# Block attention on one Trainium2 core: weight products from fp32 to three float32r products, with the weights split on the chip

## The chip, the core and the metric

One core of a Trainium2 chip runs one program. The time is the device time of one execution in microseconds; lower is better. TensorE (PE) multiplies and transposes, VectorE (DVE) and ScalarE (ACT) do elementwise work and empty the accumulation banks (PSUM), GpSimd (POOL) subtracts and issues some DMAs, SyncE (SP) issues the other DMAs.

## What is computed

Eight batches of 256 rows x 512 features, all in fp32. Layer 0 is a cross attention over features with mean and deviation outputs; the change leaves its instructions as they are. Then a transformer block of self attention, cross attention and MLP, cut to what matters here:

```
ln_out = layernorm(hidden_states, ln1_s, ln1_b)
qkv = ln_out @ w_qkv + b_qkv                     # 512 x 1536
ctx = attention(q, k, v, ltor_mask)              # 16 heads of 32
h = hidden_states + ctx @ w_ao + b_ao            # 512 x 512
q2 = layernorm(h, ln2_s, ln2_b) @ w_q + b_q      # cross: q from h
kv = encoder_states @ w_kv + b_kv                # k and v from the context
h = h + attention(q2, k2, v2, cross_mask) @ w_co + b_co
out = h + gelu(layernorm(h) @ w1 + b1) @ w2 + b2
```

## The kernel before

`build` calls `layer0`, `attention` and `mlp`. `attention` makes 16 runs in a row: run 0 to 7 are the self attention of batch 0 to 7, run 8 to 15 their cross attention. A run has 16 steps (m); a step is the scores of two heads for 128 queries. Each engine has its own instruction stream, written out by hand in this order of steps, and they meet at semaphores only.

TensorE, per step m: it waits for the exponentials of step m (`s_exp`), issues the scores of step m+2, transposes the probabilities of step m (`turn`), and on even steps multiplies them with v (`pv`). In steps 2 and 3 it transposes the normalized rows of the next run (`turn_x`), after steps 5, 9, 13 and 15 the reciprocal sums (`turn_sums`). What is left of a step carries half an `item`. Items are the weight products: q, k and v of the next run and the output product of the previous run, two items each (n = 0, 1), eight a run. Each item fills the one bank IB, which must be emptied before the next item starts (`s_free`). Before: v1 at m=1, out0 at 3, out1 at 5, q0 at 7, k0 at 9, q1 at 11, k1 at 13, v0 at 15 (part 0 of an item is done in the step before its m). Item products are fp32 matmuls: q and k 4 x 128x128 weights against 256 rows per half (L870); v with 128 rows as weights against 256 columns of the weight matrix, so that v item n covers half of the features of both row blocks (L875); out with 128 rows of `heads` against 512 columns (L883).

VectorE, per step m: `maxima` of step m+2 (L961 and two L966, which also leave the row maxima), copies of `probT` at m%4=0, reciprocals at m%4=3, `layer_norm` at m=0, `values` (v plus bias), `residual` at m=3 and 5 (L1002, L1004), `keep_rows` at m=5 and 7 (L76 to L81: statistics of the new rows and their copies into X and moments), `high_parts` (L989) of a q or k item, and the division by the sums into `heads` (L1070). Before a cross run it makes `off` from the mask in two dependent instructions (`mask_off`, L948, L950).

ScalarE, per step m: the exponentials of step m+1 (L1083), `probT` copies in the other steps, `take_x` at m=2 and 3 (L1106: scale and bias of the layer norm, bank to `xT`), `take` of a q or k item (L1097), and the spreading of the reciprocal sums (L1115, L1122).

POOL subtracts the high part of each q or k item from the whole (L1175) and issues four DMAs per item; SP issues eight (L785). These DMAs build `q_stack` and `k_stack`, 96 rows of high and low parts, from which `scores` is one float32r matmul (L823). The stacks of item n=1 are first needed by the scores of step 8. SP also loads weights and masks: `w_cross` as 4 MB and eight masks in run 0.

The MLP already uses float32r: each fp32 product is three products of high parts and rests (L1272 with 256 moving columns, L1285 with 512), with the weights split on ScalarE (L1320), VectorE (L1361) and POOL (L1349).

Of the kernel before, what the change touches and what calls it, by code (L numbers as in the profile page):

```python
# [7 lines left out]
F32 = mybir.dt.float32  # L8
# [6 lines left out]
P = 128  # L15
NB = 8
# [55 lines left out]


def keep_rows(eng, links, g, batch, s, rows, six, two):

    eng.bn_stats(six[:], rows).then_inc(links.sem, 1)  # L76
    eng.wait_ge(links.sem, links.after())
    eng.tensor_scalar(g["X"][:, batch, s, :], rows, 1.0, None, ALU.mult)
    eng.bn_aggr(two[:], six[:]).then_inc(links.sem, 1)
    eng.wait_ge(links.sem, links.after())  # L80
    eng.tensor_scalar(g["moments"][:, batch, s, :], two[:], 1.0, None, ALU.mult).then_inc(links.sem, 1)  # L81
    eng.wait_ge(links.sem, links.after())
# [18 lines left out]
def layer0(nc, d, g):  # L101
# [25 lines left out]
    with ExitStack() as ctx:  # L127
# [95 lines left out]
        with nc.Block() as block:  # L223
            @block.sync
            def _(eng):
# [25 lines left out]
                for dst, src in ((g["gb"], d["gb"]), (g["b_feat"], d["b_feat"]), (g["b1"], d["b1"]),  # L251
                                 (g["w_self"], d["w_self"])):
                    eng.dma_start(dst[:], src).then_inc(s_big, DMA)
# [418 lines left out]
def attention(nc, d, g):  # L672
# [5 lines left out]
    AHEAD = [("q", 0), ("k", 0), ("v", 0), ("q", 1), ("k", 1)]  # L678

    def weights_of(run):  # L680

        w, wo = (g["w_self"], g["wo_self"]) if run < NB else (g["w_cross"], g["w_cross"][:, :, 3 * D:4 * D])
        return {"q": w[:, :, 0:D], "k": w[:, :, D:2 * D], "v": w[:, :, 2 * D:3 * D], "out": wo}

    def item_at(run, m):

        if m == 1 and run < RUNS:
            return ("v", 1, run)
        if m in (3, 5) and run:
            return ("out", m // 5, run - 1)  # L690
        at = {7: ("q", 0), 9: ("k", 0), 11: ("q", 1), 13: ("k", 1), 15: ("v", 0)}
        if m in at and run + 1 < RUNS:
            return at[m] + (run + 1,)
        return None

# [4 lines left out]
    with ExitStack() as ctx:  # L700
# [6 lines left out]
        mask = sb("mask", [P, NB + 1, SB, S])  # L707
        off = sb("off", [P, SB, S])
        ctxT = sb("ctxT", [P, DC, S])
        xn = sb("xn", [P, SB, D])  # L710
        xT = sb("xT", [P, DC, S])
# [4 lines left out]
        v = sb("v", [P, SB, D])  # L716
# [8 lines left out]
        heads = sb("heads", [P, NG, S])  # L725
        part = sb("part", [P, D])
        six = sb("six", [P, 6])
        two = sb("two", [P, 2])
# [3 lines left out]
        s_w = sem("w")  # L732
        s_in = sem("in")
# [6 lines left out]
        s_x = sem("x")  # L740
        s_item = sem("item")
# [20 lines left out]
        s_link = sem("link")  # L762

# [29 lines left out]
        with nc.Block() as block:  # L793
            @block.sync
            def _(eng):
# [728 lines left out]
```

## Time and profile before

| | us |
|---|---|
| median of 3 runs (lowest to highest) | 1943.78 (1942.11 to 1946.71) |
| profiled execution, its own time | 1945.68 |
| its span | 1943.9 |
| TensorE busy (matmuls) | 1811.0, 93% |
| VectorE busy | 1300.8, 67% |
| ScalarE busy | 993.7, 51% |
| GpSimd busy | 346.2, 18% |

The attention runs from about 760 to 1550 us of the span. Times in rows are microseconds from the start of the span unless marked ns. PE is the matmuls, PEld the weight loads, which overlap them; the ends of matmuls are modelled, so the distance from start to start is the surer measure. A name such as `L870` is a line of the kernel before. Merged rows of a timeline show how many records they hold (x8).

### The profile page before, as it was taken

How to read it: one execution, taken by the hardware profiler on the slowest of the kernel's cores; microseconds unless marked ns; L12 is line 12 of the kernel's file. 1: busy time of each engine (PE TensorE's matmuls, PEld its weight loads, DVE VectorE, ACT ScalarE, POOL GpSimd, SP SyncE). 2: the span in 40 equal slices, each digit the busy share in tenths (PEclk: the TensorE clock that was granted, in tenths of full speed). 3: DMA queues.
4: the chain of work that ended last, by engine and by line, in shares of the span. 5: the costliest groups of instructions: out<-in, count | busy, mean ns of one | idle time of the engine just before them, and what ended most of it. 6: DMA issues, size and time to landing. Idle time of an engine off the chain costs nothing. (4 is left out here: it accounts for less than half of the span.)

```text
span 1943.9 us, 32814 instructions
## 1 busy us (share of the span) xinstructions
PE 1811.0 (93%) x11744; PEld 1179.6 (61%) x11744; DVE 1300.8 (67%) x2733; ACT 993.7 (51%) x2227; POOL 346.2 (18%) x397
## 2 busy tenths in 40 slices
PE   6999999999999982899999999999999879999998
PEld 2333333333333321777777777777777569999998
DVE  4678788887878731688888788788888653333332
ACT  1555665655666551566666666666666552111111
POOL 0001112111112113322223232222222040000000
PEclk7899999999999975999999999999999989999999
DMA  3001011110100001722232223233333050000000
GB/s 150 31 16 46 14 46 27 35 49 13 48 14 26 27 13 68 234 63 69 68 73 72 62 72 81 67 80 79 77 81 83 8 173 18 11 11 11 11 11 22
DMA packets 71936, 104.93 MB, mean 54 GB/s; under 512 B 21104, under 2 KB 35952, under 8 KB 71152
## 3 DMA queue, kind: packets, MB, share of 16 engines
q1 hardware_dynamic: 63600, 86.27, 15.7%
q0 software_dynamic: 8192, 16.79, 3.6%
q8 instruction: 83, 1.36, 0.3%
q14 instruction: 61, 0.50, 0.1%
HBM read 39.55 MB, written 4.72 MB: 23 GB/s over the span
## 5 line engine op out<-in xcount | busy, mean ns | idle before, releaser
L427 DVE TENSOR_REDUCE nmax<-ps 128x2 f32<-128x1024 f32 x256 | 311.3, 1220 | 137.4 <-PE ps L325 136.4
L559 ACT ACTIVATE prob<-ps 128x1024 f32<-128x1024 f32 x256 | 261.7, 1022 | 226.0 <-PE ps L337 225.7
L1083 ACT ACTIVATE at_prob<-at_t,at_nmax 128x256 f32<-128x256 f32 x512 | 255.7, 503 | 180.0 <-DVE at_nmax L966 178.2
L352 PE MATMUL ps<-prob,v 128*64 128x512 f32 x1024 | 287.1, 640 | 0.0
L966 DVE CUSTOM_DVE_ANT_0 at_t<-at_t,at_off 128x256 f32<-128x256 f32 x512 | 229.8, 485 | 8.8
L325 PE MATMUL ps<-k,q 32*128 32x512 f32 x1024 | 196.1, 462 | 18.3 <-DVE k L415 7.9
L325 PEld LDWEIGHTS ps<-k,q 32*128 32x128 f32 x1024 | 84.8, 191 | 193.1 <-issue 109.9
L961 DVE SCALAR_TENSOR_TENSOR at_t<-ps,at_mask 128x512 f32<-128x512 f32 x256 | 175.0, 683 | 31.3 <-PE ps L823 28.7
L1337 ACT ACTIVATE mlp_h<-ps,b 128x256 f32<-128x256 f32 x128 | 53.7, 472 | 269.4 <-PE ps L1272 269.2
L1376 DVE CAST mlp_h_hi<-mlp_h 128x512 fp32r<-128x512 f32 x64 | 29.3, 458 | 220.9 <-ACT mlp_h L1337 220.9
L1175 POOL TENSOR_TENSOR at_low<-at_low,at_high 128x512 fp32r<-128x512 f32 x64 | 81.4, 1271 | 515.7 <-DVE at_high L989 450.2
L823 PE MATMUL ps<-at_k_stack,at_q_stack 96*128 96x256 f32 x512 | 153.4, 382 | 10.6 <-ACT at_prob L1083 9.8
L835 PE MATMUL ps<-ident,at_prob 128*128 128x128 f32 x1024 | 155.7, 274 | 1.1 <-ACT at_prob L1083 1.1
L1272 PE MATMUL ps<-mlp_x_hi,mlp_w_hi 128*128 128x256 f32 x512 | 145.6, 284 | 7.5 <-DVE mlp_w_lo L1361 7.5
L1272 PE MATMUL ps<-mlp_x_lo,mlp_w_hi 128*128 128x256 f32 x512 | 145.6, 284 | 0.0
L1272 PE MATMUL ps<-mlp_x_hi,mlp_w_lo 128*128 128x256 f32 x512 | 145.5, 284 | 0.0
L337 PE MATMUL ps<-q,k 32*128 32x512 f32 x512 | 131.4, 509 | 11.0 <-ACT prob L559 10.7
L870 PE MATMUL ps<-at_xT,w_self 128*128 128x256 f32 x512 | 128.7, 397 | 6.1 <-ACT at_low L1097 3.4
L835 PEld LDWEIGHTS ps<-ident,at_prob 128*128 128x128 f32 x1024 | 119.4, 141 | 1.6 <-ACT at_prob L1083 1.6
L823 PEld LDWEIGHTS ps<-at_k_stack,at_q_stack 96*128 96x128 f32 x512 | 92.1, 192 | 44.0 <-issue 22.8
L1149 ACT ACTIVATE at_probT<-ps 128x512 f32<-128x512 f32 x192 | 111.6, 581 | 7.8 <-PE ps L835 7.8
L352 PEld LDWEIGHTS ps<-prob,v 128*64 128x64 f32 x1024 | 51.9, 138 | 98.0 <-issue 97.1
(138 smaller groups left out, 3496.3 us busy)
## 6 DMA issues: line engine op xcount, KB each, us to landing
at_k_stack<-at_high SPq DMA_DIRECT2D x256, 64.0 KB, 2.1
at_q_stack<-at_high SPq DMA_DIRECT2D x128, 64.0 KB, 2.7
at_q_stack<-at_high POOLq DMA_DIRECT2D x128, 64.0 KB, 2.4
at_q_stack<-at_low SPq DMA_DIRECT2D x128, 64.0 KB, 2.3
at_k_stack<-at_low POOLq DMA_DIRECT2D x128, 64.0 KB, 2.3
mlp_w_in<-in_w SPq DMA_DIRECT2D x32, 256.0 KB, 3.0
c_in<-in_ctx SPq DMA_DIRECT2D x8, 512.0 KB, 4.2
X<-in_x SPq DMA_DIRECT2D x8, 512.0 KB, 4.9
```

Of the source, the lines that this page charges most:

```text
L325: mm = eng.matmul(ps[:, SC + 2 * (N % 2) + i, :], lhsT[r, slot, P * j:P * (j + 1)], rhs[r, n % RING, :], start=(half == 0), stop=(half == 1))
L337: mm = eng.matmul(ps[:, ST + i, :], lhsT[r, n % RING, P * c:P * (c + 1)], rhs[r, slot, :], start=(half == 0), stop=(half == 1))
L352: mm = eng.matmul(ps[2 * QD * k:2 * QD * (k + 1), VB, :], v[:, c, HG * G + 2 * p + k, :], prob[:, M % PROBS, k, :], start=(c == 0), stop=( ...
L427: eng.tensor_reduce(nmax[:, n % 2, j, 2 * p:2 * p + 2], ps[:, at:at + 2, :], AX, ALU.max, negate=True).then_inc(s_max, 1)
L559: eng.activation(prob[:, M % PROBS, :, :], ps[:, ST:ST + 2, :], ACT.Exp).then_inc(s_exp, 1)
L823: mm = eng.matmul(ps[:, SC + p, S * i:S * (i + 1)], q_stack[:, 2 * p + i, T, P * j:P * (j + 1)], k_stack[:, 2 * p + i, T, :], start=True, ...
L835: mm = eng.transpose(ps[:, PT + m % 2, P * k:P * (k + 1)], prob[:, m % 2, i, P * c:P * (c + 1)], ident[:])
L870: mm = eng.matmul(bank[:, S * T:S * (T + 1)], w[:, c, P * (2 * n + T):P * (2 * n + T + 1)], src[:, c, :], start=(c == 0), stop=(c == DC - 1))
L961: eng.scalar_tensor_tensor(out=t[:, i, :, :], in0=ps[:, SC + i, :].rearrange("p (h k) -> p h k", h=2), scalar=-SCALE, in1=mask[:, mask_of( ...
L966: ins = eng.tensor_tensor_reduce(t[:, i, k, :], t[:, i, k, :], off[:, j, :], 1.0, NEVER, ALU.add, ALU.min, nmax[:, m % 4, k:k + 1])
L1083: ins = eng.activation(prob[:, m % 2, i, :], t[:, p, i, :], ACT.Exp, scale=-1.0, bias=nmax[:, m % 4, i:i + 1], accum_out=z[:, T % 2, j, 2 ...
L1272: mm = eng.matmul(ps[:, HB + n % 2, S * i:S * (i + 1)], w[:, c, col], x[:, c, :], start=(k == 0), stop=(k == len(terms) - 1))
```

## The change

- Products of q, k, v and out become float32r: W x = W_hi x_hi + W_hi x_lo + W_lo x_hi (`TERMS`), three matmuls for one. In run 0 the q, k and v products stay fp32 (`whole`).
- v is made by token blocks: item n is 128 rows against all 512 columns, and `v` has two buffers, one for each parity of the run.
- Weights: ScalarE copies the fp32 weights to `w_hi` (which rounds them), VectorE writes `w_lo = w_raw - w_hi` over `w_raw`, in pieces of 128 x 512 placed by `pieces_at`. Self weights are split in run 0, q, k and v of the cross weights in run 7 and their out weights in run 8. The cross weights are loaded over the self weights' rests, by role and after the last self item of that role.
- Activations: `take_x` writes `x_hi` and the whole x (over `xn`), `low_x` the rest; the context is split by `high_context` and `low_context`, the head outputs by `high_heads` and `low_heads`.
- Order of items: k1 at m=1 of its own run, out0 3, out1 5, q0 7, k0 9, v0 11, v1 13, q1 15.
- `keep_rows` goes: `residual` writes X in place, `statistics` writes `moments` directly. `mask_off` is one instruction. Masks have two buffers instead of nine and are loaded one per cross run.
- The DMA of the self out weights comes behind the first stacks.

```diff
-    AHEAD = [("q", 0), ("k", 0), ("v", 0), ("q", 1), ("k", 1)]
+    AHEAD = [("q", 0), ("k", 0), ("v", 0), ("v", 1), ("q", 1)]
+    TERMS = ((0, 0), (0, 1), (1, 0))
...
+    def pieces_at(run, m):
+
+        if run in (0, NB - 1) and m in (3, 4, 5, 6, 8, 9):
+            role, c = {3: (0, 0), 4: (0, 2), 5: (1, 0), 6: (1, 2), 8: (2, 0), 9: (2, 2)}[m]
+        elif run in (0, NB) and m in (10, 11):
+            role, c = 3, 2 * (m - 10)
+        else:
+            return []
+        return [(0 if run == 0 else 1, role, c), (0 if run == 0 else 1, role, c + 1)]
...
+                        if name == "out":
+                            eng.wait_ge(s_hlo, NG * run + 2)
+                        if name == "q":
+                            eng.wait_ge(s_x if run == 0 else s_xlo, 2 if run == 0 else 2 * run)
+                        if name == "k" and run >= NB:
+                            eng.wait_ge(s_clo, 2 * (run - NB) + 2)
...
-                                mm = eng.matmul(bank[:, S * T:S * (T + 1)], w[:, c, P * (2 * n + T):P * (2 * n + T + 1)],
-                                                src[:, c, :], start=(c == 0), stop=(c == DC - 1))
...
+                                for k, (a, z_) in enumerate(TERMS):
+                                    mm = eng.matmul(out, w[a][:, c, col], src[z_][:, c, :],
+                                                    start=(c == 0 and k == 0), stop=(c == DC - 1 and k == 2))
...
+                            for k, (z_, a) in enumerate(TERMS):
+                                mm = eng.matmul(bank, src[z_][:, c, rows], w[a][:, c, :],
+                                                start=(c == 0 and k == 0), stop=(c == DC - 1 and k == 2))
...
+                def low_x(run, n):
+
+                    eng.wait_ge(s_x, 2 * run + n + 1)
+                    half = slice(2 * n, 2 * n + 2)
+                    eng.tensor_tensor(x_lo[:, half, :], xn[:, :, S * n:S * (n + 1)], x_hi[:, half, :].bitcast(F32),
+                                      ALU.subtract).then_inc(s_xlo, 1)
...
+                def low_weights(layer, role, c):
+
+                    if layer == 0 and c == 0 and role < 3:
+                        made(eng, ROLES[role], 1, 0)
+                    eng.wait_ge(s_whi, 4 * (4 * layer + role) + c + 1)
+                    eng.tensor_tensor(weights(1, role)[:, c, :], weights(2, role)[:, c, :],
+                                      weights(0, role)[:, c, :].bitcast(F32), ALU.subtract).then_inc(s_wlo, 1)
...
+                        if m in (4, 5) and run + 1 < RUNS:
+                            low_x(run + 1, m - 4)
+                        if m in (6, 7) and NB <= run + 1 < RUNS:
+                            low_context(run + 1, m - 6)
+                        if m in (0, 1) and run:
+                            low_heads(run - 1, 2 + m)
+                        if m in (8, 12):
+                            low_heads(run, m // 4 - 2)
+                        if m:
+                            for x in pieces_at(run, m - 1):
+                                low_weights(*x)
...
+                    for c in range(2 * n, 2 * n + 2):
+                        for dst in (x_hi[:, c, :], raw_x(c))[run == 0:]:
+                            ins = eng.activation(dst, ps[:, TB, S * (c % 2):S * (c % 2 + 1)], ACT.Identity,
+                                                 bias=gb[:, 1, c:c + 1], scale=gb[:, 0, c:c + 1])
...
+                        if m in (5, 6) and NB <= run + 1 < RUNS:
+                            high_context(run + 1, m - 5)
+                        if m in (7, 11, 15):
+                            high_heads(run, m // 4 - 1)
+                        if m == 0 and run:
+                            high_heads(run - 1, 3)
+                        for x in pieces_at(run, m):
+                            high_weights(*x)
```

On SP, the loads of the cross weights (four DMAs of 256 KB for each role) stand between and behind the stacks of run 7: q's between the stacks of q1 and k1, k's and v's behind k1's; the out weights' stand in front of the stacks of run 9.

## Rows read from the trace of the kernel before

**Rows 1.** The page's forty slices, matmuls, busy tenths.
```profile
PE   6999999999999982899999999999999879999998
```
**Rows 2.** Stretches: from:to, length, busy PE, PEld, DVE, ACT, POOL, granted clock, DMA.
```profile
971.30:1017.80 46.50, 46.38 (x355) 36.77 (x353) 38.31 (x112) 30.33 (x96) 12.96 (x21) 1.00 0.29 69
...
1308.20:1355.90 47.70, 46.48 (x355) 36.85 (x354) 39.34 (x114) 30.35 (x96) 13.03 (x21) 1.00 0.32 78
...
786.90:831.50 44.60, 39.81 (x295) 33.20 (x295) 32.39 (x97) 28.60 (x89) 14.75 (x22) 0.96 0.71 225
```
**Rows 3.** Waits in one self run: who waited for whom, us, times, longest.
```profile
ACT at_prob L1083 <- DVE at_nmax L966: 11.0, 8, 2.4
```
**Rows 4.** Timeline of TensorE in self runs: start, us, engine, line, operation.
```profile
961.31 2.00 PE L870 MATMUL ps<-at_xT,w_self 128*128 128x256 f32 x8
...
962.96 0.59 PE L823 MATMUL ps<-at_k_stack,at_q_stack 96*128 96x256 f32 x2
...
985.87 0.81 PE L823 MATMUL ps<-at_k_stack,at_q_stack 96*128 96x256 f32 x2
...
987.82 0.19 PEld L883 LDWEIGHTS ps<-wo_self,at_heads 128*128 128x128 f32 x1 [0.24 <-issue]
...
988.25 0.19 PEld L883 LDWEIGHTS ps<-wo_self,at_heads 128*128 128x128 f32 x1 [0.24 <-issue]
...
994.80 0.48 PE L823 MATMUL ps<-at_k_stack,at_q_stack 96*128 96x256 f32 x2
```
**Rows 5.** Timeline of TensorE in the MLP, float32r products of 256 and 512 columns.
```profile
1742.27 0.28 PE L1272 MATMUL ps<-mlp_x_hi,mlp_w_hi 128*128 128x256 f32 x1
...
1745.15 0.63 PE L1285 MATMUL ps<-mlp_w_hi,mlp_h_hi 128*128 128x512 f32 x2
...
1747.89 0.28 PE L1272 MATMUL ps<-mlp_x_hi,mlp_w_hi 128*128 128x256 f32 x1
```
**Rows 6.** VectorE groups, 740 to 1480 us: busy, mean ns, idle before them.
```profile
L1070 DVE TENSOR_TENSOR at_heads<-ps,at_rz_wide 128x256 f32<-128x256 f32 x57 | 23.9, 418 | 10.7 <-ACT at_rz_wide L1122 10.7
...
L1004 DVE TENSOR_TENSOR at_part<-X,at_part 128x512 f32<-128x512 f32 x28 | 19.4, 692 | 1.0
...
L78 DVE TENSOR_SCALAR X<-at_part 128x512 f32<-128x512 f32 x27 | 11.5, 427 | 0.9
...
L950 DVE TENSOR_SCALAR at_off<-at_off 128x512 f32<-128x512 f32 x8 | 10.1, 1257 | 0.3
...
L81 DVE TENSOR_SCALAR moments<-at_two 128x2 f32<-128x2 f32 x27 | 4.6, 169 | 0.9
```
**Rows 7.** Timeline of maxima and POOL's subtraction; last row durations ns min/median/max.
```profile
882.17 0.67 DVE L961 SCALAR_TENSOR_TENSOR at_t<-ps,at_mask 128x512 f32<-128x512 f32 x1
...
883.58 0.20 DVE L1041 RECIPROCAL at_rz<-at_z 128x8 f32<-128x8 f32 x1
...
961.87 1.27 POOL L1175 TENSOR_TENSOR at_low<-at_low,at_high 128x512 fp32r<-128x512 f32 x1 [2.43 <-DVE at_high L989]
...
962.35 1.07 DVE L966 CUSTOM_DVE_ANT_0 at_t<-at_t,at_off 128x256 f32<-128x256 f32 x1
...
L966 DVE CUSTOM_DVE_ANT_0 at_t<-at_t,at_off x512: 411/423/1545, 788.2 to 1539.8; 128x256 f32<-128x256 f32 x171
```
**Rows 8.** ScalarE groups in attention; last row the MLP's weight copy, ns min/median/max.
```profile
L1106 ACT ACTIVATE at_xT<-ps,gb 128x256 f32<-128x256 f32 x64 | 32.3, 557 | 3.8 <-PE ps L894 3.8
...
L1115 ACT ACTIVATE at_rz_cols<-at_rz 128x256 f32<-128x256 f32 x57 | 23.4, 410 | 3.2 <-DVE at_rz L1041 3.2
...
L1320 ACT ACTIVATE mlp_w_hi<-mlp_w_in x32: 627/632/657, 1564.2 to 1605.5; 128x512 fp32r<-128x512 f32 x32
```
**Rows 9.** A q or k item's way into the stacks, timeline and the page's DMA issues.
```profile
965.75 0.84 ACT L1097 ACTIVATE at_low<-ps,b_feat 128x256 f32<-128x256 f32 x2 [0.31 <-PE ps L870]
...
975.87 5.04 SPq L785 DMA_DIRECT2D at_k_stack<-at_high  x8
...
at_k_stack<-at_high SPq DMA_DIRECT2D x256, 64.0 KB, 2.1
```
**Rows 10.** DMA issues of run 0: operation, count, KB each, us to landing.
```profile
w_cross<-in_w_cross SPq DMA_DIRECT2D x1, 4096.0 KB, 13.9
```

More of the change, by code:

```diff
@@ L71, in after @@
         return self.base + self.n
[L74 to L82, printed above, removed]
 def linked_batches(eng, sem, body, before, per):
@@ new lines, in item @@
+                    if n == 0 and 0 in parts:
+                        if run in ((0, NB) if name == "out" else (1, NB)):
+                            eng.wait_ge(s_wlo, 4 * (4 * layer + role) + 4)
+                        if name == "out":
[4 more added lines that the diff above has]
+                            eng.wait_ge(s_clo, 2 * (run - NB) + 2)
@@ L867, in item @@
+                    if name == "out":
+                        if n == 0 and 1 in parts:
+                            eng.wait_ge(s_hlo, NG * run + 4)
+                        src = (h_hi, h_lo)
+                    else:
+                        src = (x_hi, x_lo) if name == "q" or run < NB else (c_hi, c_lo)
+                    w = weights(0, role), weights(1, role), weights(2, role)
+                    whole = run == 0 and name != "out"
                     if name in "qk":
                         for T in parts:
+                            out, col = bank[:, S * T:S * (T + 1)], slice(P * (2 * n + T), P * (2 * n + T + 1))
@@ L1003, in residual, with statistics @@
                     taken(eng, "out", s, run)
-                    eng.tensor_tensor(part[:], X[:, run % NB, s, :], part[:], ALU.add).then_inc(s_part, 1)
+                    eng.tensor_tensor(rows, rows, g["b_row"][:, 2 * (run // NB) + 1, :], ALU.add).then_inc(s_part, 1)
+                def statistics(run, s):
                     eng.wait_ge(s_part, 2 * run + s + 1)
+                    eng.bn_stats(six[:], X[:, run % NB, s, :]).then_inc(links.sem, 1)
+                    eng.wait_ge(links.sem, links.after())
+                    eng.bn_aggr(moments[:, run % NB, s, :], six[:]).then_inc(links.sem, 1)
+                    eng.wait_ge(links.sem, links.after())
@@ L1067, in _ @@
                             eng.wait_ge(s_pv, UNITS * run + 2 * G + 2)
-                            if G == 0 and run:
-                                made(eng, "out", 1, run - 1)
-                            eng.tensor_tensor(heads[:, G, :], ps[:, OB + G % 2, 0:S], rz_wide[:], ALU.mult).then_inc(s_norm, 1)
-                        if m in (7, 9, 11, 13) and run + 1 < RUNS:
-                            high_parts(run + 1, "kq"[m // 2 % 2], (m - 7) // 4)
+                            if 4 * run + G >= 2:
+                                eng.wait_ge(s_hlo, NG * run + G - 1)
+                            eng.tensor_tensor(h_raw[:, G % 2, :], ps[:, OB + G % 2, 0:S], rz_wide[:], ALU.mult).then_inc(s_norm, 1)
+                        x = item_at(run, m)
+                        if x and x[0] in "qk":
+                            high_parts(x[2], x[0], x[1])
+                        if (run, m) == (0, 1):
+                            made(eng, "k", 1, 0)
+                            layer_norm(1)
+                low_heads(RUNS - 1, 2)
+                low_heads(RUNS - 1, 3)
                 for s in range(SB):
                     residual(RUNS - 1, s)
-                    keep_rows(eng, links, g, NB - 1, s, part[:], six, two)
+                    statistics(RUNS - 1, s)
             @block.scalar
```

213 lines of the change are left out of this document (130 added, 83 removed).

## Prediction

> **What bounds the kernel now.** I read the page's forty slices first [rows 1]: from slice 17 to 31, the attention part, the matmul row stands at 9. Then busy time by stretch [rows 2], at the full granted clock (1.00, which is 2.4 GHz): one self run (one batch, 16 steps) lasts 46.5 us with TensorE busy 46.38, VectorE 38.31, ScalarE 30.33; a cross run lasts 47.7 us with 46.48, 39.34, 30.35. Then the waits inside one self run [rows 3]: ScalarE waits 11.0 us for VectorE's maxima, while TensorE is idle for 0.1 us (46.5 less 46.38). So TensorE is the bound, and VectorE has some 8 us of room; but the exponentials wait for it already. A cross run is 1.2 us longer than a self run at equal TensorE work: it has one thing more in VectorE's stream before the maxima of the next run, `mask_off`, whose second instruction takes 1.26 us [rows 6]. VectorE is thus already able to hold TensorE up.
>
> **TensorE's work, part by part.** An fp32 matmul leaves two records: half a q or k item is four matmuls, and its row has x8. Two records of 512 columns have their loads 0.43 us apart (987.82, 988.25 [rows 4]), so such a matmul costs 0.86 and half an `out` item, two of them, 1.72. At 256 columns a record is half that, 0.215, and the eight of half a q item 1.72; from 961.31 to the next pair of scores at 962.96 the trace has 1.65, with the last record's end under that pair. The new products are in the MLP already [rows 5]: 24 float32r matmuls of 256 columns from 1742.27 to 1745.15, 0.12 each; 12 of 512 columns from 1745.15 to 1747.89, 0.228 each.
> q and k: half an item becomes 12 x 0.12 = 1.44, less by 0.28; eight halves, 2.3 us a run. v: two items of 2 x 4 matmuls of 256 columns (four halves, 6.9 us) become two of four products x 3 of 512 columns, 24 x 0.228 = 5.5; less by 1.4. out: 8 x 0.86 = 6.9 becomes 24 x 0.228 = 5.5; less by 1.4. Together 5.2 us a run, so 46.4 becomes about 41.2 in a self run. MLP and layer 0 aren't touched.
> The Trainium skill (FP8 and Floating Point Precision, TensorE Precision Notes) says that true fp32 makes four passes through the array; three single passes would then save a quarter of the 27.5 us, 6.9 and not 5.2. The rows give 0.36 against 0.43 and 0.68 against 0.86, so about a fifth at most, and the rows decide.
>
> **VectorE's work.** Added to each run: `low_x`, two subtractions of 512 columns, 0.69 us each by `at_part<-X,at_part`; `low_heads`, four of 256 columns, 0.42 each by `at_heads`; in cross runs `low_context`, two more of 0.69 [rows 6]. Removed: the copies in `keep_rows`, 2 x (0.43 + 0.17), the second for the moments, and in cross runs one `mask_off` instruction, 1.26 [rows 6]. Self: 1.38 + 1.68 - 1.2 = +1.9, so 38.3 becomes 40.2. Cross: +1.9 + 1.4 - 1.3 = +2.0, so 39.3 becomes 41.3. TensorE's 41.2 and VectorE's 40.2 to 41.3 are now the same size, in two streams that wait for each other in every step. This is what takes part of the gain.
>
> **Where they meet.** One step of maxima is 1.41 us in VectorE's stream (882.17 to 883.58 [rows 7]); exponentials of one step need another 1.0 after it. TensorE issues scores two steps ahead, so VectorE may lag some two steps (5.2 us) less scores, maxima, exponentials and hand-overs (about 3.0), an estimate of 2.2 us. Estimates from the same rows for VectorE's steps 3 to 5: 3.05 (maxima 1.41, reciprocal 0.2, residual 0 in two of 0.69 with hand-overs), 2.6 (maxima, a copy and low_x of 0.6 each) and 4.4 (maxima, statistics 0.9, residual 1, low_x), 10.1 us. TensorE had 8.93 us for these steps (985.87 to 994.80 [rows 4]) and saves three halves of `out`, 3 x 0.36 by the numbers above: 7.9; and residual 0 can't begin before TensorE ends step 3. Laid out by hand from there, TensorE waits for the exponentials about 0.7 us at step 8, 0.2 at 12, 0.4 and 0.2 at steps 3 and 4 of the next run, where layer_norm, two low_heads and the high part of k1 lie close together. With some 0.7 of hand-overs that I can't place, 2.2 us: a self run is 41.2 + 0.1 + 2.2 = 43.5. In a cross run low_context adds 1.2 in steps 6 and 7, which VectorE hasn't caught up by step 10: 44.6. The bounds of the waiting are 0.7 (step 8 alone) and 4.
>
> **ScalarE.** `take_x` doubles, four more of 0.56; four `high_heads`, bounded by `at_rz_cols`, 0.41; two high_context of 0.63 in cross runs, by the MLP's weight copy [rows 8]. 30.3 + 2.2 + 1.6 = 34.1, or 35.4: below 43, so nothing, except that step 2's doubled take_x lets turn_x of step 3 wait 0.1 to 0.3 (in the 0.7 above).
>
> **k1 is moved** from step 13 of the run before to step 1, and `scores` of step 8 are issued in step 6. Its chain: take 0.84 [rows 9], high part 0.43 (a copy of L78's shape [rows 6]), POOL's subtraction 1.27 [rows 7], 0.4 of hand-overs, eight issues on SP 5.04 and the landing 2.1 [rows 9], 10.1 us. The cover is TensorE's steps 2 to 5, the 7.9 above and about 3.2 for step 2, 11.1 us. VectorE reaches that high part some 1 to 2 us late by my layout, so the stack lands at about the time it is wanted; up to 0.7 of lateness hides in the wait that step 8 has anyhow, so I take nothing, and up to 2.5 for the range. q1 (13 to 15) has more room. SP's queue is free by then, as q1's eight issues end before; POOL's own four come after the same subtraction. The v buffer is doubled, so its wait on the run before goes. wo moves behind the first stacks, the masks are read one at a time: nothing, with the 4 MB of w_cross gone from run 0.
>
> **The splits.** Run 0 gets 16 pieces: ScalarE 0.63 each [rows 8], VectorE 0.69 by L1004 [rows 6]. VectorE had 32.4 busy in run 0's 44.6 us [rows 2]; it becomes 32.4 + 1.4 (low_x) + 0.8 + 11.0 = 45.6, and with waits, which I put at 2.0 as in a later run, 47.6: +3.0. Run 7 gets 12 pieces, 12 x 0.61 (start to start) = 7.3, and q's weights are loaded in front of k1's stack: 4 MB took 13.9 us to land [rows 10], so 1 MB 3.5, of which I take half on the path: 43.5 + 7.3 + 1.7 = 52.5 against 46.5, +6.0. Run 8: 44.6 + 4 x 0.61 = 47.0 against 47.7, -0.7. Run 15 has no items of a next run: -2. The tail: out less 1.4, low_heads and high_heads plus 0.8, copies less 0.6: -1.
>
> **The sum.** Six self runs (1 to 6) x -3.0 = -18.0; six cross runs (9 to 14) x -3.1 = -18.6; +3.0 + 6.0 - 0.7 - 2 - 1 = +5.3. Total -31.3 us. The profiled execution took 1945.68 (span 1943.9), so 1914.4; it is 1.9 above the median of the runs shown, 1943.78, so 1912.5 for the median, which I give as 1912.
>
> **The rivals.**
> TensorE stays the bound: VectorE's lag fits in its slack. For it: TensorE's row is full now and the average VectorE load stays at or below 41.3. Against: steps 3 to 5. Runs of 42.0 and 42.4: 6 x -4.5 + 6 x -5.3 = -58.8, + 5.3, gives 1890.
> The gain is eaten by waiting: each run waits the upper 4 us and one more in cross runs, 45.2 and 46.3; 12 x -1.35 + 5.3 = -11: 1933. For it: ScalarE waits 11.0 us a run for maxima already.
> Slower, by the k1 chain and the port: POOL's subtraction of 1.27 us stretches a maxima instruction from 0.42 to 1.07 when both run [rows 7], while L961, which reads PSUM, stays at 0.68. Every subtraction added to VectorE reads two SBUF tensors. If each of POOL's four costs up to 1.12 instead of 0.65 (worst L966: 1.55 against 0.42 [rows 7]), that is 1.9 a run; it delays k1's high part, and past a delay of 1.1 us its chain is longer than its cover and TensorE stands still at step 6, up to 2.5: 43.5 + 4.4 = 47.9 and 49.0, +1.35 x 12 + 5.3: 1965. It decides once VectorE is over 2 us late in step 1. The Trainium skill (GPSIMD Engine Reference, Specifications) says that GpSimd shares its SBUF interfaces with VectorE and that instructions with two SBUF inputs contend, which is a rule against this change; the rows agree for the maxima, and none shows the new subtractions beside POOL.
> The products don't come at the MLP's price: beside fp32 work they are held to their weight loads, 0.19 us each [rows 4] instead of 0.12. Then q and k cost 2.28 a half against 1.72, +4.5 on eight halves against -2.9 on v and out: TensorE's work rises by 1.6 a run, to 48.1 and 49.3; 12 x 1.6 + 5.3 gives 1968. Against it: the MLP has the same loads and keeps 0.12.
>
> **Chances.** Forecast 0.52 (its own range 1900 to 1926), TensorE bound 0.20, gain eaten 0.16, slower by k1 and port 0.10, price of products 0.02. 0.2% of this time, 3.9 us, is about what a measurement can tell from none. Of the eaten case a quarter lies within it: same 0.04; slower 0.12; faster 0.84. The range takes in the first three, with their bounds: 1884 to 1942.
>
> **What would show it.** Self runs of 43 to 44 us with TensorE busy 41 of them and waits of `ps L823` for `at_prob`; float32r records 0.12 and 0.228 apart in attention; VectorE busy 40 us a run; run 7 the longest, over 50. A wait of L823 for DMA k_stack of over 1 us a run is the slow case; runs near 42 the fast one. The prediction is wrong if the layout of steps 3 to 8 is: it is made by hand, and a microsecond a run is 15 us in the end.

## The result and the profile after

The changed kernel takes 1977.3 us, median of 4 (1973.1 to 1982.9), the kernel before on the same chip 1945.2 (1942.1 to 1951.9): a ratio of 1.016 [1.0125, 1.020]. It is slower by 1.6%, where 1912 and faster was predicted. The profiled execution took 1977.97, its span is 1976.2.

The page of the changed kernel: busy time by engine, then TensorE's busy tenths and the granted clock in forty slices.

```profile
PE 1766.4 (89%) x12216; PEld 1188.9 (60%) x12216; DVE 1348.7 (68%) x2802; ACT 1067.1 (54%) x2399; POOL 347.9 (18%) x397
...
PE   6999999999999964798999868889989879999998
...
PEclk7999999999999967899999988999999979999999
```

TensorE's total fell from 1811.0 us to 1766.4, but its slices 18 to 31 (of 40, the first is 1), solid nines before [rows 1], now have six eights and one six: the work is less and the holes are more. Some of these 1766.4 us were also done at a lower clock.

Stretches of the changed kernel, from the first scores of a run to those of the next (from:to, length, busy PE, PEld, DVE, ACT, POOL, granted clock, DMA share, GB/s): run 0, self runs 2 and 3, run 7, run 8, cross run 10.

```profile
785.30:836.30 51.00, 40.71 (x303) 34.38 (x303) 42.69 (x114) 37.68 (x109) 13.23 (x20) 0.83 0.36 96
...
885.00:931.70 46.70, 42.16 (x385) 36.09 (x385) 39.51 (x114) 33.45 (x104) 13.07 (x20) 1.00 0.29 69
931.70:980.00 48.30, 43.76 (x388) 37.65 (x385) 39.75 (x115) 33.59 (x104) 13.09 (x20) 0.96 0.28 67
...
1125.30:1187.60 62.30, 46.14 (x387) 39.32 (x386) 48.88 (x128) 40.74 (x118) 13.08 (x20) 0.92 0.38 102
1187.60:1242.00 54.40, 45.49 (x388) 38.90 (x386) 42.76 (x117) 36.37 (x110) 13.08 (x20) 0.91 0.36 93
...
1292.90:1341.10 48.20, 43.66 (x387) 37.61 (x386) 41.42 (x117) 34.66 (x106) 13.07 (x20) 0.96 0.33 83
```

Against [rows 2]: a self run of 46.5 us became 46.7 where the clock stayed at its upper level (2.4 GHz) and 48.3 where it fell, though TensorE's busy time is 42.2 in place of 46.4. VectorE is busy 39.5 to 39.8, as predicted (40.2). Where the 34 us between first and last scores come from, in the two profiled executions:

| runs | before | after | difference | predicted |
|---|---|---|---|---|
| 1 to 6 | 283.2 | 289.0 | +5.8 | -18.0 |
| 9 to 14 | 290.0 | 292.3 | +2.3 | -18.6 |
| 0 | 44.6 | 51.0 | +6.4 | +3.0 |
| 7 | 46.6 | 62.3 | +15.7 | +6.0 |
| 8 | 47.7 | 54.4 | +6.7 | -0.7 |
| 15 and the tail | 39.0 | 36.3 | -2.7 | -3 |

So two questions: what stands in a steady run where 3 us were to be gained, and why the runs that split weights cost 29 us and not 8. The waits of TensorE in the attention part show both (who waited for whom: us in all, times, longest).

```profile
PE ps L927 <- DVE at_x_lo L1071: 27.7, 13, 2.1
...
PE ps L949 <- ACT at_xn L1207: 22.8, 16, 1.4
PE ps L864 <- ACT at_prob L1183: 22.4, 25, 4.2
...
ACT at_c_hi L1218 <- DMA at_c_raw<-in_ctxT: 13.4, 7, 7.0
...
PE ps L961 <- ACT at_rz_cols L1240: 9.9, 15, 0.7
PE ps L937 <- DVE w_lo L1092: 9.1, 2, 4.8
...
PE ps L927 <- DVE w_lo L1092: 5.1, 3, 2.7
...
ACT at_w_hi L1233 <- DMA w_raw<-in_w_cross: 3.8, 1, 3.8
...
PE ps L864 <- DMA at_k_stack<-at_high: 1.2, 4, 0.6
```

The first is q's products (L927) waiting for `low_x`, the second `turn_x` (L949) waiting for the doubled `take_x`, the third scores waiting for exponentials. The fourth and the eighth are ScalarE standing until loads have landed, of the context in run 8 and of q's cross weights in run 7. The fifth is `turn_sums` (L961) waiting for `widen`, ScalarE's spreading of the reciprocals, the sixth and seventh are products waiting for rests of weights. The last is the k1 chain, which costs next to nothing. The prediction has only `at_prob` and `at_xn` among its waits of a steady run, the second as 0.1 to 0.3 us.

In time the first looks like this in run 3, TensorE's timeline and then VectorE's over the same microseconds.

```profile
956.50 0.64 PE L889 MATMUL ps<-at_probT,at_v 128*32 128x128 f32 x16
959.28 0.36 PE L927 MATMUL ps<-at_x_hi,at_w_hi 128*128 128x256 f32 x1 [2.14 <-DVE at_x_lo L1071]
959.48 0.28 PE L927 MATMUL ps<-at_x_lo,at_w_hi 128*128 128x256 f32 x1
959.60 0.28 PE L927 MATMUL ps<-at_x_hi,w_lo 128*128 128x256 f32 x1
...
960.10 0.41 PE L927 MATMUL ps<-at_x_hi,at_w_hi 128*128 128x256 f32 x1
960.31 0.41 PE L927 MATMUL ps<-at_x_lo,at_w_hi 128*128 128x256 f32 x1
```
```profile
956.18 0.69 DVE L1062 BATCH_NORM_STATS2 at_six<-X 128x6 f32<-128x512 f32 x1
956.90 0.18 DVE L1064 BATCH_NORM_AGGREGATE moments<-at_six 128x2 f32<-128x6 f32 x1
957.12 0.69 DVE L1055 TENSOR_TENSOR X<-ps,X 128x512 f32<-128x512 f32 x1
957.85 0.69 DVE L1057 TENSOR_TENSOR X<-X,b_row 128x512 f32<-128x512 f32 x1
958.45 0.68 DVE L1071 TENSOR_TENSOR at_x_lo<-at_xn,at_x_hi 128x512 fp32r<-128x512 f32 x1
```

In step 6 TensorE has the products of q0 next at about 957.1. The second `low_x` stands behind statistics and residual in VectorE's step 5 and ends at 959.1. TensorE stands idle for 2.14 us (the row at 956.50 holds sixteen matmuls, the last of which starts at 956.87). At 960.10 the products go from 0.12 to 0.21 apart: the granted clock has fallen to its lower level (1.2 GHz) at 960.02 and stays there for 3.4 us. From the first scores to the last there are 15 half-clock stretches with 71.7 us in all (before: 4 with 13.7). The wait is there in 13 runs, 1 to 6 and 8 to 14, and in ten of them, all but 2, 6 and 13, a half-clock stretch begins near its end, from 0.3 us before the products to 1.3 behind their start. The half-clock stretch in step 5 of run 7 comes with a wait of 4.2 us for exponentials.

### The profile page after: what moved, and what is told of

Same layout as the page of the kernel before. It is cut to its first block and busy times, and to the rows that moved or that the text cites. A ratio compares the mean times of both kernels' runs of the same rounds, so it can differ in the third digit from the quotient of the medians.

```text
span 1976.2 us, 33999 instructions
## 1 busy us (share of the span) xinstructions
PE 1766.4 (89%) x12216; PEld 1188.9 (60%) x12216; DVE 1348.7 (68%) x2802; ACT 1067.1 (54%) x2399; POOL 347.9 (18%) x397
## 5 line engine op out<-in xcount | busy, mean ns | idle before, releaser
L1019 DVE CUSTOM_DVE_ANT_0 at_t<-at_t,at_off 128x256 f32<-128x256 f32 x512 | 238.3, 502 | 8.8
L1014 DVE SCALAR_TENSOR_TENSOR at_t<-ps,at_mask 128x512 f32<-128x512 f32 x256 | 174.7, 682 | 34.3 <-PE ps L864 33.6
L876 PE MATMUL ps<-ident,at_prob 128*128 128x128 f32 x1024 | 161.6, 282 | 1.4 <-ACT at_prob L1183 1.4
L927 PE MATMUL ps<-at_x_hi,at_w_hi 128*128 128x256 f32 x352 | 112.3, 319 | 30.5 <-DVE at_x_lo L1071 27.7
L864 PE MATMUL ps<-at_k_stack,at_q_stack 96*128 96x256 f32 x512 | 118.2, 314 | 23.8 <-ACT at_prob L1183 22.4
L876 PEld LDWEIGHTS ps<-ident,at_prob 128*128 128x128 f32 x1024 | 124.6, 145 | 1.9 <-ACT at_prob L1183 1.9
L864 PEld LDWEIGHTS ps<-at_k_stack,at_q_stack 96*128 96x128 f32 x512 | 86.9, 200 | 46.9 <-ACT at_prob L1183 37.6
```

The costliest lines, as they stand in the source:

```text
L864: mm = eng.matmul(ps[:, SC + p, S * i:S * (i + 1)], q_stack[:, 2 * p + i, T, P * j:P * (j + 1)], k_stack[:, 2 * p + i, T, :], start=True, ...
L876: mm = eng.transpose(ps[:, PT + m % 2, P * k:P * (k + 1)], prob[:, m % 2, i, P * c:P * (c + 1)], ident[:])
L1014: eng.scalar_tensor_tensor(out=t[:, i, :, :], in0=ps[:, SC + i, :].rearrange("p (h k) -> p h k", h=2), scalar=-SCALE, in1=mask[:, mask_of( ...
L1019: ins = eng.tensor_tensor_reduce(t[:, i, k, :], t[:, i, k, :], off[:, j, :], 1.0, NEVER, ALU.add, ALU.min, nmax[:, m % 4, k:k + 1])
```

## The experiments

Each ratio is to the kernel before, which took 1945.6 to 1946.1 us beside the experiments.

**The wait of q0 for `low_x`, and the clock.** First without the rest in q's products: their second term takes the high part in place of the rest (so q leaves out W_hi x_lo), and only k of self runs waits for `low_x`. The number of products and VectorE's work stay.

```diff
-                            eng.wait_ge(s_x if run == 0 else s_xlo, 2 if run == 0 else 2 * run)
+                            eng.wait_ge(s_x, 2 * run + 2)
+                        if name == "k" and 0 < run < NB:
+                            eng.wait_ge(s_xlo, 2 * run)
...
-                                    mm = eng.matmul(out, w[a][:, c, col], src[z_][:, c, :],
+                                    mm = eng.matmul(out, w[a][:, c, col], src[0 if name == "q" else z_][:, c, :],
```

> The changed kernel, but every q product takes the high parts of x where it took the rests (same number and size of float32r products, the result of q lacks its rest term), so item q0 waits for take_x only and k0 waits for the rests. VectorE does all its work in the same order. Theory W (the wait of q0 in step 6 for low_x(1), 2.1 us a run in 13 of the runs, costs itself and makes the clock fall for 3.4 us): q0 then starts when residual 1 has emptied the bank, some 0.8 us late instead of 2.2, and the half-clock stretch of each run goes: self run 48.3 to about 45.3, total 1977 to about 1937. Rival V (VectorE's load of 40 to 41 us with its hand-overs is the bound, the wait only shows it): VectorE's stream is the same, so the run stays within 1 us of 48.3 and the wait turns up at the next exponentials; total above 1965.

Measured: 1962.7 us, ratio 1.009 [1.006, 1.012]. Self runs 1 to 5 are 45.6 to 46.4 us and none of them has a half-clock stretch; so the clock followed the wait, and the forecast for a self run held. The total's (1937) did not. It took 3 us for each of 13 runs; runs 1 to 5 gave 11.0 us together, cross runs 9 to 14 only 4.4, and runs 6, 7 and 8 nothing (49.5, 62.5 and 54.5). Of the wait of q0, 0.7 us is left, for the bank that the second `residual` empties.

Second, the whole computation, with VectorE's order changed: both `low_x` in step 4, the residual ahead of the statistics.

```diff
-                        if m in (5, 7) and run:
-                            statistics(run - 1, m // 2 - 2)
                         if m in (3, 5) and run:
                             residual(run - 1, m // 2 - 1)
-                        if m in (4, 5) and run + 1 < RUNS:
-                            low_x(run + 1, m - 4)
+                        if m in (5, 7) and run:
+                            statistics(run - 1, m // 2 - 2)
+                        if m == 4 and run + 1 < RUNS:
+                            low_x(run + 1, 0)
+                            low_x(run + 1, 1)
```

> The changed kernel with both low_x in step 4 of VectorE, and in step 5 residual 1 before statistics 0; nothing is left out. Theory W: low_x(1) is done some 2 us before TensorE's step 6, residual 1 empties the bank 0.9 us earlier than now, q0 doesn't wait at all, no half-clock stretch: self run 48.3 to 44.5 or 45, total about 1977 - 13 x 3.5 = 1932. Rival V: the work is only shifted, maxima of step 5 come 0.6 us later, run within 1 us of before, total above 1965.

Measured: 1965.1 us, ratio 1.010 [1.006, 1.013], where 1932 was forecast: the gain in the cross runs is again small. A self run and a cross run of it, and a wait:

```profile
929.70:975.80 46.10, 42.65 (x386) 36.13 (x385) 40.00 (x115) 33.45 (x105) 13.08 (x20) 1.00 0.29 70
1331.40:1378.40 47.00, 42.66 (x386) 36.14 (x384) 41.25 (x117) 34.40 (x106) 13.07 (x20) 1.00 0.34 85
...
PE ps L927 <- DVE at_c_lo L1078: 7.8, 6, 1.4
```

TensorE's step 6 is 3.4 us where it was 5.1 to 6.3, and the granted clock is 1.00. The last row is the same fault one step on: in cross runs k0 now waits for the rests of the context, which VectorE makes behind other work too. My 44.5 to 45 for a self run was too low by 1: the waits of steps 15 and 3 (0.7 and 1.4 us) remain, and 0.4 at q0. With run 2 of the changed kernel, whose clock did not fall, the cost can be parted. Its steps 6 to 8 take 5.14, 2.11 and 2.88 us against 3.39, 2.75 and 2.99 here: the late q0 costs 1.0 net, 1.75 in step 6, of which the next two steps give back 0.75 (0.5 of waiting for exponentials between them falls away). Runs 3 to 5 with the same wait and the fall are 48.1 to 48.3 where run 2 is 46.7: the half-clock stretch costs 1.4 to 1.6 us more.

**The bank that `take_x` holds.** `take_x` read each transposed block twice from PSUM, so `turn_x` of the next step found the bank full. Here it reads the bank once, whole, and makes the high part by one copy of 512 columns from SBUF after the bank is free. The waits of `turn_x`, `turn_sums` and run 0's q go over to the new semaphore `s_xw`, and `low_x` counts `s_x` without run 0; these lines are left out here.

```diff
-                        for dst in (x_hi[:, c, :], raw_x(c))[run == 0:]:
-                            ins = eng.activation(dst, ps[:, TB, S * (c % 2):S * (c % 2 + 1)], ACT.Identity,
-                                                 bias=gb[:, 1, c:c + 1], scale=gb[:, 0, c:c + 1])
-                    ins.then_inc(s_x, 1)
+                        ins = eng.activation(raw_x(c), ps[:, TB, S * (c % 2):S * (c % 2 + 1)], ACT.Identity,
+                                             bias=gb[:, 1, c:c + 1], scale=gb[:, 0, c:c + 1])
+                    ins.then_inc(s_xw, 1)
+                    if run:
+                        eng.wait_ge(s_xw, 2 * run + n + 1)
+                        eng.activation(x_hi[:, 2 * n:2 * n + 2, :], xn[:, :, S * n:S * (n + 1)], ACT.Copy).then_inc(s_x, 1)
```

> The changed kernel with take_x as two activations from the bank (whole x) and then one copy of 512 columns from SBUF for the high parts; the bank is free for the next turn_x after the first two. Theory W2 (turn_x of step 3 waits 1.4 to 1.7 us a run for the doubled take_x): wait falls by 0.9 us or goes, step 3 of 4.17 us becomes 3.3 or less; alone it may be given back in step 6, where q0 waits for the rests whose halves now come a little later: run 48.3 to 47.4, total about 1963; if the step 6 wait takes it all, 1975. Rival: ScalarE's total matters, one copy of 0.63 against two activations of 0.56: no more than 0.5 us a run.

Measured: 1964.6 us, ratio 1.009 [1.006, 1.012], as expected. A self run of it, and what is left of the wait:

```profile
932.20:979.70 47.50, 43.89 (x385) 37.55 (x385) 39.69 (x115) 33.00 (x102) 13.07 (x20) 0.96 0.28 68
...
PE ps L950 <- ACT at_xn L1207: 9.2, 16, 1.2
```

Step 3 went from 4.17 to 3.27 us and the run from 48.3 to 47.5; the 22.8 us of waiting are 9.2, and the fall of the clock in step 6 stays. Then both edits together:

> lowx_first and bank_free together. Two waits in series in one run (1.4 us in step 3 on ScalarE, 2.1 us in step 6 on VectorE): if they are separate, the gains add: self run 48.3 - 2.7 - 0.9 = 44.7, cross 46.2, total about 1952. If VectorE's load (40 busy in 44.7) has become the bound by then, the second gain is given back: self run stays at 45.6, total 1963.

Measured: 1956.0 us, ratio 1.0055 [1.0035, 1.0075], self runs 1 to 5 of 44.7 to 45.6. In these runs the gains add: 10.6 and 4.4 us singly, 14.3 together. Over the whole kernel they are 21.3 us together, and 12.2 and 12.7 singly.

**The runs that split weights.** In the changed kernel SyncE's queue at the start of run 8's loads reads:

```profile
1208.21 0.58 SPq L823 DMA_DIRECT2D at_mask<-in_mask_cross  x1
1211.65 1.77 SPq L819 DMA_DIRECT2D wo_raw<-in_w_cross  x4
1213.46 0.43 SPq L827 DMA_DIRECT2D at_c_raw<-in_ctxT  x1
```

The out weights may only be loaded once the last self `out` item has read the old ones, in step 5, and the context of batch 1 waits behind them though nothing holds it. ScalarE, which splits it, then stands 7.0 us (the row of `at_c_hi` above), and the exponentials queue behind it: TensorE waits 3.5 us for them in step 7. The experiment exchanges the two.

```diff
-                    if run == NB + 1:
-                        load_weights(3)
...
+                    if run == NB + 1:
+                        load_weights(3)
```

> The changed kernel with SyncE loading the context of run 9 before the out weights, whose load waits for the last out item of run 7 in step 5 of run 8. Theory: ScalarE's wait of 7.0 us for the context in run 8 goes, and with it the rest of that run's excess: run 8 from 54.4 to about 50, total 1977 to 1972. Rival (the excess of run 8 is the four pieces of weights, not the load): run 8 stays at 54, total unchanged within 2 us.

Measured: 1971.1 us, ratio 1.012 [1.009, 1.016], and run 8 went from 54.4 to 49.6 us. For runs 0 and 7 the suspicion was the other way round: the pieces reach VectorE after the products that need them. In the next kernel they start two steps earlier in run 0 and follow without a gap in run 7, and q's new weights are loaded ahead of q1's stacks (a line moved in SyncE's stream).

```diff
-        if run in (0, NB - 1) and m in (3, 4, 5, 6, 8, 9):
-            role, c = {3: (0, 0), 4: (0, 2), 5: (1, 0), 6: (1, 2), 8: (2, 0), 9: (2, 2)}[m]
+        if run == 0 and 1 <= m <= 6:
+            role, c = (m - 1) // 2, (m - 1) % 2 * 2
+        elif run == NB - 1 and 3 <= m <= 8:
+            role, c = (m - 3) // 2, (m - 3) % 2 * 2
```

> The changed kernel with the weight pieces one to three steps earlier in run 0 (q in steps 1 and 2, k 3 and 4, v 5 and 6, where v was in 8 and 9) and the v pieces one step earlier in run 7, and with q's cross weights loaded before the q1 stack of run 7. Deadline theory (TensorE waits for VectorE's rests of v's weights because they are made in the step in which v0 needs them, 4.3 us in run 0, 4.8 in run 7, each with a fall of the clock): run 0 from 51.0 to 47, run 7 from 62.3 to about 56, total 1977 to 1967. Load theory (16 and 12 pieces of 0.69 us on a full VectorE are the excess): run 0 and run 7 change by less than 2 us together.

Measured: 1968.9 us, ratio 1.012 [1.010, 1.014]. Run 0 is 47.6 us in place of 51.0, run 7 54.3 in place of 62.3. The waits of its run 7 (L929 and L939 are the products, L927 and L937 in the changed kernel, which has 4.7 and 4.8 us there and 3.8 for the DMA):

```profile
PE ps L929 <- DVE w_lo L1094: 3.8, 1, 3.8
PE ps L939 <- DVE w_lo L1094: 1.4, 1, 1.4
ACT at_w_hi L1235 <- DMA w_raw<-in_w_cross: 0.8, 1, 0.8
```

VectorE's busy time in run 7 is the same, 48.9 and 48.4: the 8.0 us were not the work but when its inputs and results come. How much of it is the pieces and how much the load wasn't parted, since the edit moves both. In the changed kernel TensorE waits 4.2 us in step 5 of run 7 for exponentials, which queue on ScalarE behind its 3.8 us wait for q's cross weights, and then 2.0, 2.7 and 4.8 us for rests. In the edited kernel the 4.2 are gone, and 3.8 and 1.4 are left.

**All of it.** The four edits together, and `low_context` ahead of residual and statistics so that k0 of cross runs doesn't wait:

> lowx_first, bank_free, context_first and pieces_early together, and in cross runs the rests of the context ahead of statistics 1 in step 7, where k0 waits for them in step 8 by 1.2 us. If the waits were the loss: self runs 44.7, cross runs 45.5, run 0 47, run 7 55, run 8 48; total 1943.8 + (44.6-46.5) x 5.. summed over the runs about 1930, faster than the kernel before. If VectorE's load is the bound behind them: self runs 45.6, cross 47, total 1950, slower than before.

Measured: 1932.3 us (6 runs), ratio 0.993 [0.991, 0.995]: it beats the kernel before. Singly the edits gave 12.2, 12.7, 6.3 and 8.4 us, 39.6 in sum, and together 45.0 with the fifth, which wasn't run by itself. Its stretches of a self run, a cross run, run 0 and run 7:

```profile
927.70:972.50 44.80, 42.42 (x384) 36.07 (x385) 39.36 (x114) 32.60 (x102) 13.11 (x20) 1.00 0.31 72
1306.40:1352.30 45.90, 42.85 (x383) 36.07 (x384) 40.84 (x117) 33.59 (x104) 13.10 (x20) 1.00 0.35 87
789.70:836.70 47.00, 40.12 (x301) 33.42 (x302) 42.27 (x113) 37.17 (x107) 13.29 (x20) 0.85 0.40 105
1109.40:1162.90 53.50, 44.09 (x387) 37.59 (x386) 48.67 (x130) 40.63 (x118) 13.10 (x20) 0.97 0.42 119
```

**What the products themselves save.** In this kernel, built from the changed one, each product of runs 1 to 15 is one fp32 matmul of the high parts; the rests are made and waited for but left out of the products.

```diff
-                                for k, (a, z_) in enumerate(TERMS):
-                                    mm = eng.matmul(out, w[a][:, c, col], src[z_][:, c, :],
-                                                    start=(c == 0 and k == 0), stop=(c == DC - 1 and k == 2))
+                                mm = eng.matmul(out, w[0][:, c, col].bitcast(F32), src[0][:, c, :].bitcast(F32),
+                                                start=(c == 0), stop=(c == DC - 1))
```

> The changed kernel with all splits, waits and places as they are, but each weight product of runs 1 to 15 as one fp32 matmul of the high parts (the rests are left out of the result). It prices the float32r products by themselves. My sum has 5.2 us of TensorE's work a run; with the same waits in steps 3 and 6 a self run goes from 48.3 to about 51.5, a little less than 5.2 because longer steps hide part of the waits; total about 2025. If VectorE were the bound, the products would not matter: run 48 to 49, total below 1990.

Measured: 2009.6 us, ratio 1.033 [1.031, 1.035], where 2025 was expected. Its runs 3 and 11:

```profile
940.50:990.30 49.80, 46.57 (x339) 33.70 (x338) 39.87 (x114) 33.48 (x104) 13.00 (x20) 1.00 0.27 65
1366.00:1415.80 49.80, 46.57 (x339) 33.70 (x338) 41.51 (x117) 34.59 (x106) 13.00 (x20) 1.00 0.33 80
```

That is 1.5 us over the 48.3 of the changed kernel and not 3.2, as the fall of the clock is gone here. Against its run 2, at equal clock, it is 3.1. But the waits are shorter here: TensorE is idle for 3.2 us of this run (49.8 less 46.57) and for 4.5 of run 2 (46.7 less 42.16). So the products by themselves are worth 4.4 us, the difference of the busy times, of which longer steps hide 1.3; the kernel before and run 2 differ by 4.2 (46.38 and 42.16). The ends of matmuls are modelled, so these are estimates. The forecast was 5.2. What is missing shows in the timeline of half an `out` item, here in the kernel `widen` described below:

```profile
939.02 0.48 PE L940 MATMUL ps<-at_wo_hi,at_h_hi 128*128 128x512 f32 x1
939.33 0.39 PE L940 MATMUL ps<-wo_lo,at_h_hi 128*128 128x512 f32 x1
939.56 0.39 PE L940 MATMUL ps<-at_wo_hi,at_h_lo 128*128 128x512 f32 x1
...
940.49 0.45 PE L867 MATMUL ps<-at_k_stack,at_q_stack 96*128 96x256 f32 x2
940.77 0.60 PE L879 MATMUL ps<-ident,at_prob 128*128 128x128 f32 x4
```

The pitch is 0.23 as forecast, but the first of each half is 0.31 to 0.34 ahead of the second (q and k: 0.12, and the first 0.19 to 0.22). For 16 halves that is some 1.4 us. From the first product to the transposes behind the scores it is 1.75 us; in the kernel before the same stretch is 1.96 (its L883 at 984.55, L835 at 986.51). So this half of `out` saves 0.21, where 0.36 was in the sum. Another, in step 4, goes from 2.06 to 1.73 (990.45 to 992.51 before, 905.28 to 907.01 in the changed kernel) and saves 0.33: what half an item saves depends on its place. At 256 columns the stretch was 1.97 (v, L875 at 980.98, L835 at 982.95) and is 1.77 (q in `widen`, 956.38 to 958.15).

**`turn_sums` and q1.** The change put q1's `take` into ScalarE's step 15, ahead of `widen`, for whose reciprocals TensorE waits in that step. The next kernel is the one with all edits, and `widen` ahead of `take` in step 15.

```diff
+                        if m == STEPS - 1:
+                            widen(run, NG - 1)
                         x = item_at(run, m)
                         if x and x[0] in "qk":
                             take(*x)
-                        if m % 4 == 0 and m or m == STEPS - 1:
+                        if m % 4 == 0 and m:
```

> Kernel all_five with the widening of the reciprocals of the last head group put ahead of q1's half on ScalarE in step 15. Theory that turn_sums waits in that step for work that the new order put in front of it: step 15 of a steady run goes from 3.7 us to 3.0 to 3.2, runs become 0.6 us shorter, total about 1923. Rival, that the time is given back because q1 then comes late: steps 16 or 0 become as much longer and the total stays at 1930 to 1934.

Measured: 1921.9 us (1921.4 to 1925.8), ratio 0.988 [0.987, 0.990], the fastest of this study. Step 15 went from 3.70 to 2.97 us. The wait of L961 for `at_rz_cols` is gone from TensorE's list. Its run 4, and two waits of TensorE in run 3 (44.5 us) that are left:

```profile
970.80:1015.00 44.20, 42.41 (x384) 36.06 (x385) 39.43 (x114) 32.58 (x102) 13.07 (x20) 1.00 0.31 73
```
```profile
937.16 0.50 PE L867 MATMUL ps<-at_k_stack,at_q_stack 96*128 96x256 f32 x2 [0.49 <-ACT at_prob L1187]
...
941.90 0.63 PE L952 MATMUL ps<-ident,at_xn 128*128 128x128 f32 x4 [0.52 <-ACT at_xn L1210]
```

**v by blocks or by halves of the features.** All edits, with v computed by feature halves again (24 products of 256 columns for an item in place of 12 of 512):

```diff
+                                for k, (z_, a) in enumerate(TERMS):
+                                    mm = eng.matmul(out, src[z_][:, c, rows], w[a][:, c, col],
+                                                    start=(c == 0 and k == 0), stop=(c == DC - 1 and k == 2))
```

> Kernel all_five with v computed by halves of the features again (256 columns a product) instead of by token blocks (512 columns), still three float32r products. By the pitches of the MLP rows the halves are 0.3 us a run dearer: total about 1936. By the pitches that the changed kernel's own rows show, 0.34 us for the first product of each block's group against 0.20, the feature halves are 0.1 to 0.15 us cheaper each: 0.5 us a run, total about 1925.

Measured: 1936.3 us, ratio 0.996 [0.994, 0.998]; and on top of `widen`:

> Both edits on top of all_five. If they are independent and both theories hold, about 1917; if either gives nothing, 1923 to 1926; if both give nothing, 1932.

Measured: 1927.2, ratio 0.991 [0.989, 0.993]. Both medians are 4 to 5 us above the kernels with token blocks, where the second theory, that halves are cheaper, wanted one 7 us below: it has fallen. The size of the first isn't shown either. The intervals of the ratios overlap at their ends in both pairs, steps 10 to 12 take 2.97, 2.21, 2.97 us by halves and 2.94, 2.25, 2.94 by blocks, and runs 1 to 5 sum to 226.7 against 225.6 us, with `widen` to 223.8 against 223.1. In both pairs of profiles run 6 is 1.6 to 1.7 us longer by halves, and has a half-clock stretch then and none by blocks; from the first scores of run 0 to those of run 15 the profiles differ by 2.3 us and, with `widen`, by 0.1. Why the medians differ stays open.

## Why the prediction was wrong, step by step

**What bounds the kernel** was read rightly: TensorE was full [rows 2], and less work for it opened room in the run. How much room, and who would stand in it, was not. (The row of nines begins at slice 18, not 17; nothing hangs on it.)

**TensorE's work** (5.2 us a run): the pitches of [rows 5] hold in attention, 0.12 and 0.23, so the rival that holds the products to their weight loads did not happen. The term was mis-sized in that 12 or 6 pitches were taken for half an item: the first product of a half takes 0.08 to 0.11 more. TensorE's busy time fell by 4.2 us, and rose by 4.4 when the fp32 products came back. The Trainium skill's four passes for true fp32 (FP8 and Floating Point Precision, TensorE Precision Notes) would have made the saving 6.9, farther off still; the measurement decides. That is 1 us a run and some 13 us of the 65 by which the time was missed. In the MLP rows such groups stand back to back with one another; in attention each stands between transposes and scores.

**Where they meet** is the step that failed. The layout by hand has `low_x` of the second half at the end of VectorE's step 5, behind statistics and residual; but it followed VectorE only for its maxima, and asked whether the exponentials come late. That q0 of step 6 needs that same subtraction (the diff has the wait on `s_xlo`) was left out. The wait of 2.1 us costs a steady run 1.0, and 2.4 to 2.6 where the clock falls with it. The exponentials, for which 2.2 us a run were set aside, take 0.3 (run 2 of the changed kernel) to 1.0 (`widen`): the order of size was found, for a wait that isn't the main one.

**ScalarE**: "step 2's doubled take_x lets turn_x of step 3 wait 0.1 to 0.3" is the right mechanism with the wrong size, 1.4 us of waiting and 0.9 of step 3. Its four activations stand 0.45 from start to start, 1.8 us, behind the exponentials and a copy of the same step. "Below 43, so nothing" is the second fault: the average load of an engine was taken as proof that nothing on it is late. Moving q1 to step 15 put 0.8 us of `take` in front of `widen`; that a moved item's `take` passes `widen` on ScalarE's queue was not looked at, and costs 0.6 us a run. VectorE's own sums came out: 39.5 to 39.8 us busy in a self run and 41.4 in a cross run, for 40.2 and 41.3.

The ledger of a self run, for run 2 at the full clock: TensorE busy 42.2, and idle 0.3 for exponentials, 1.4 for `take_x`, 2.1 for `low_x` and 0.7 for `widen`, gives 46.7, as measured. The forecast was 41.2, 0.1 and 2.2, 43.5. The half-clock stretch makes 48.3 of 46.7. Without the waits that could be moved it is 44.2 (run 4 of `widen`), 42.4 busy and 1.8 idle. That the 2.2 set aside for waiting come near these 1.8 is luck: only 1.0 of them are waits for exponentials.

**The k1 chain** takes nothing, as forecast: 1.2 us in all, four times. The slower rival that was built on it did not happen; slower came from elsewhere. **The port**: the maxima beside POOL's subtraction stretch again (61 of 512, median 1.08 us against 0.42), but none of the 30 `low_x` (681 ns) nor of the 64 `low_heads` (413 ns) fell beside POOL's subtraction, so what a subtraction costs there stays open. The rule of the Trainium skill on the shared interfaces (GPSIMD Engine Reference, Specifications) agrees with the maxima and wasn't put to the test by the new work.

**The splits**: VectorE's busy time was not the fault, 42.7 us in run 0 where 45.6 was forecast. Its use was. The 7.3 of run 7 priced pieces as work added to a full engine, and the load at 1.7; in fact scores wait 4.2 us for exponentials that stand behind that load, and products of q, k and v wait for single pieces, 0.4 to 4.8 us at a time. With the holes of 4.2 to 4.8 us goes a half-clock stretch, with those of 2.0 and 2.7 none; the clock is 0.92 over run 7 and 0.83 over run 0, whose stretch was 0.96 before [rows 2]. Moving the pieces and the load, with the same work, gave back 3.4 and 8.0 us: run 0 then has the 47.6 that were forecast, run 7 54.3 against 52.5. Run 8 was forecast at 47.0 from its pieces alone; the context's load behind the out weights' on SyncE's queue was overlooked, 4.8 us.

**The sum**: from -31 to +32. Products some +13, the waits of steady runs (`take_x`, `low_x`, `widen`) and the clock, less the 2.2 set aside, some +32, the three runs +20. The three cases in the range, which ended at 1942, differ only in how long TensorE waits for exponentials, and the two slower rivals were left out of it; a range from bounds is only as wide as the list of things that can be late.

## What to carry to other kernels

When work is moved off the bound engine onto others, follow each new intermediate from its producer's place in the queue to its first consumer, and compare the two times; the engines' averages (39.5 of 46.7 us here) say nothing of it. Then look at what a copy into a shared bank, a load queued on one engine and a moved item hold up in front of others. When TensorE gets less work in the same steps, a hole of 2 us stands in a dense stream, and has to be priced with what the clock may do beside it (here in ten of 13 cases).

## What the runs showed of the hardware

- The granted clock. In the changed kernel q0 waits up to 2.1 us in step 6 of 13 runs, 2.41 us between starts in run 3, and in ten of them the clock goes to 1.2 GHz close to the start of the products (959.28 and 960.02 in run 3), in nine of the ten for 3.4 us; a self run is then 1.4 to 1.6 us longer than run 2, which has the same gap and no fall. With the gap at 0.4 us (step 6 of 3.4 us), the falls are gone from runs 1 to 5 and 10 to 14. In the kernel of one fp32 matmul for each product step 6 still waits 1.5 us and these runs keep the full clock.
- The first float32r product of a group, behind transposes or the products with v, takes 0.19 to 0.22 (256 columns) or 0.31 to 0.34 us (512) to the second, in place of 0.12 or 0.23; behind an idle gap of 2.1 us it is 0.19 too. What makes it so wasn't tried.
- Three float32r products against one fp32: 4.2 us less of TensorE's busy time for 16 halves of an item; by timelines 0.20 to 0.33 for one, of 1.96 to 2.06.
- VectorE's instruction that reads the scores from PSUM (L1014) takes 0.68 us beside POOL's subtraction (60 times) and away from it (196 times), while the maxima from SBUF go from 0.42 to 1.08.
